# One attention stage of a fused kernel: TensorE's loop over single groups, single buffers for what it reads, and K and V projected later

## The reference, cut to what matters

```python
x = _layernorm(x + _attn(x, x, x, ..., True), ln1_g, ln1_b)
x = _layernorm(x + _attn(x, encoder_output, encoder_output, ..., False), ln2_g, ln2_b)
x = _layernorm(x + _moe(x, router_w, router_b, e_w1, e_b1, e_w2, e_b2), ln3_g, ln3_b)
```

```python
Q = (q_in @ wq + bq).reshape(Bq, Sq, H, HD)
Kp = (k_in @ wk + bk).reshape(Bq, Sk, H, HD)
V = (v_in @ wv + bv).reshape(Bq, Sk, H, HD)
scores = jnp.einsum('bqhd,bkhd->bhqk', Q, Kp) / jnp.sqrt(jnp.float32(HD))
a = jax.nn.softmax(scores, axis=-1)
o = jnp.einsum('bhqk,bkhd->bqhd', a, V).reshape(Bq, Sq, Dm)
return o @ wo + bo
```

## Time and profile before

| | |
|---|---|
| median of 3 runs | 1501.34 us (1499.0 to 1504.86) |
| the profiled execution's own time | 1501.08 us |
| its span, first to last instruction | 1499.4 us |
| mean granted TensorE clock | 0.933 of full |
| busy share of the span: PE, PEld, DVE, ACT, POOL | 86%, 72%, 65%, 66%, 57% |
| attention phase | first values about 24 us, last residual 564 us |
| fused stage | first bias matmul 948 us, last residual 1354 us |

### The profile page before, as it was taken

How to read it: one execution, slowest core, us unless ns; L and a number is a source line. 1 busy time by engine, 2 the same in 40 slices (tenths; PEclk the granted TensorE clock), 3 DMA queues, 4 the chain that set the end, 5 groups by cost and what they waited for, 6 DMA issues and landing times. The chain is left out here.

```text
span 1499.4 us, 59843 instructions
## 1 busy us (share of the span) xinstructions
PE 1284.4 (86%) x23136; PEld 1073.3 (72%) x23136; DVE 969.2 (65%) x2107; ACT 997.0 (66%) x2030; POOL 861.9 (57%) x1340
## 2 busy tenths in 40 slices
PE   5999999989999987679999999157887777895998
PEld 2787887778888776568999999136665556683776
DVE  4787787767878865883555555266877767762332
ACT  1778877768788852986666666166776666772554
POOL 2557766656676753108999987566555554322331
PEclk9999999999999995598999999669999999996999
DMA  3232332322322430522222223242332323212221
GB/s 102 76 103 91 98 105 91 95 87 80 89 80 88 117 90 8 176 64 63 69 68 68 68 67 65 66 106 65 84 89 68 96 64 82 66 31 57 71 70 49
DMA packets 154923, 118.91 MB, mean 79 GB/s; under 512 B 17440, under 2 KB 130592, under 8 KB 154784
## 3 DMA queue, kind: packets, MB, share of 16 engines
q1 hardware_dynamic: 146336, 99.61, 22.6%
q0 software_dynamic: 8448, 17.32, 5.1%
HBM read 78.55 MB, written 38.27 MB: 78 GB/s over the span
## 5 line engine op out<-in xcount | busy, mean ns | idle before, releaser
L831 DVE TENSOR_REDUCE at_mx<-at_ps_s 128x16 f32<-128x1024 f32 x128 | 156.1, 1220 | 106.9 <-PE at_ps_s L560 60.4
L760 ACT ACTIVATE at_pt<-at_ps_t 128x1024 f32<-128x1024 f32 x128 | 130.6, 1020 | 56.3 <-PE at_ps_t L574 55.6
L753 ACT ACTIVATE at_pr<-at_dd 128x1024 f32<-128x1024 f32 x128 | 135.2, 1056 | 34.7 <-DVE at_dd L839 34.6
L2261 ACT ACTIVATE ex_hg<-ex_ps_h,ex_wt 128x128 f32<-128x128 f32 x544 | 154.4, 372 | 1.3 <-PE ex_ps_y L2230 1.2
L2201 POOL DMA_INDIRECT ex_xg<-x,ex_ti x136 | 141.2, 1038 | 23.4 <-issue 21.8
L2282 DVE COPY ex_wt<-experts 128x1156 f32 x136 | 105.0, 774 | 75.7 <-issue 64.3
L839 DVE TENSOR_TENSOR at_dd<-at_ps_s,at_mx 128x1024 f32<-128x1024 f32 x128 | 153.8, 1203 | 0.1
L2221 PE MATMUL ex_ps_h<-ex_xt,ex_wt 128*128 128x128 f32 x1088 | 148.6, 281 | 0.0
L1611 POOL DMA_INDIRECT l_yg<-rows,l_sl x128 | 128.8, 1007 | 33.0 <-issue 30.8
L574 PE MATMUL at_ps_t<-ident,at_pr 128*128 128x128 f32 x1024 | 139.9, 280 | 5.1 <-issue 3.1
L2230 PE MATMUL ex_ps_y<-ex_wt,ex_hg 128*128 128x128 f32 x1088 | 143.6, 275 | 0.4 <-ACT ex_hg L2261 0.4
(11 more groups left out here) (239 smaller groups left out, 3282.9 us busy)
## 6 DMA issues: line engine op xcount, KB each, us to landing
rows<-ex_y SPq DMA_DIRECT2D x136, 64.0 KB
x<-at_ln_out SPq DMA_DIRECT2D x32, 256.0 KB, 3.2
at_kx<-in_xt SPq DMA_DIRECT2D x16, 256.0 KB, 2.8
at_qx<-in_xt SPq DMA_DIRECT2D x16, 256.0 KB, 2.8
at_vin<-in_xt SPq DMA_DIRECT2D x16, 256.0 KB, 2.7
at_xr<-in_x SPq DMA_DIRECT2D x16, 256.0 KB, 3.0
x1t<-at_xt SPq DMA_DIRECT2D x16, 256.0 KB, 3.2
at_kx<-in_ctxt SPq DMA_DIRECT2D x16, 256.0 KB, 2.7
```

The source lines that it names most:

```text
L753: act.activation(pr[:, p], dd[:, p], ACT.Exp, scale=SCALE).then_inc(p_ready, 1)
L760: act.activation(pt[:, 2 * h + p], ps_t[:, :, :, :], ACT.Copy).then_inc(pt_ready, 1)
L831: dve.tensor_reduce(mx[:, p], ps_s[:, :, 4 * p:4 * p + 4, :], AX.X, ALU.max).then_inc(mx_ready, 1)
L2261: ins = act.activation(hg[:, s % 2, f, :], ps_h[s % HB][:, f, :], ACT.Gelu, bias=wt[:, s % HB, B1 + f:B1 + f + 1])
```

## The change

- `kv` becomes two tiles, `kx` and `vin`, each single; `qx`, `kb`, `qb`, `ot`, `z4` and `c.vx` become single. K and V of a group are loaded by two transfers instead of one.
- TensorE's loop is `over_ones`, one step in its body, over g = 2 to 14; unrolled are g = -1, 0, 1 and 15, 16, 17. Its step is rotated (it begins with `project_out` of g-2, `turn`, `scores` of g second half).
- `project_k` is of g+1 instead of g+2. `project_v` is of g instead of g+1, and stands ahead of `scores` of g+1 first half instead of behind it.
- ScalarE: `copy_t` of the first pair is behind `mask_q`; `exponent` of pair (2g+1, 0) is behind `mask_k`; `copy_v` is of g, ahead of `exponent` of (2g+1, 1). VectorE: `recip` of the first half is ahead of `gain_own`. GpSimd: `spread` of the first half is ahead of `fetch_open`. The other moves in their steps are rotations: the same cyclic order with the step's boundary elsewhere.
- SyncE: order x, output, front (four groups ahead instead of five), `x3`, K two ahead, V one ahead.

```diff
+def over_ones(eng, step, first, end, last):
+    for g in range(first, 2):
+        step(At(1, g))
+    with eng.Fori(2, end) as m:
+        step(At(1, m, 0, m))
+    for g in range(end, last):
+        step(At(1, g))
...
-        kv = n.sb("kv", [P, 2, GT])
-        qx = n.sb("qx", [P, 2, GT])
+        kx = n.sb("kx", [P, GT])
+        vin = n.sb("vin", [P, GT])
+        qx = n.sb("qx", [P, GT])
-        kb = n.sb("kb", [P, 2, 2, GT])
-        qb = n.sb("qb", [P, 2, GB, 2, SEQ])
+        kb = n.sb("kb", [P, 2, GT])
+        qb = n.sb("qb", [P, GB, 2, SEQ])
...
+                def load_k(a):
+                    if beyond(a.g, 0):
+                        sp.wait_ge(k_ready, a.g)
+                    sp.dma_start(kx[:, :], layer.kv_src[:, bass.ts(a.place, GT)]).then_inc(in_k, 16)
...
 sync step
-                    if a.shift(2).exists():
-                        load_kv(a.shift(2))
                     if a.shift(1).exists():
                         load_x(a.shift(1))
                     if a.shift(-2).exists():
                         store_tok(a.shift(-2))
-                    if a.shift(5).exists():
-                        load_front(a.shift(5))
+                    if a.shift(4).exists():
+                        load_front(a.shift(4))
                     if a.shift(3).exists():
                         store_x3(a.shift(3))
+                    if a.shift(2).exists():
+                        load_k(a.shift(2))
+                    if a.shift(1).exists():
+                        load_v(a.shift(1))
...
 tensor step
+                    if a.shift(-2).exists():
+                        if a.shift(-1).exists():
+                            pe.wait_ge(vx_ready, g)
+                        else:
+                            pe.wait_ge(y_ready, g - 2)
+                        project_out(a.shift(-2))
+                    if a.shift(-1).exists():
+                        turn(g * 2 - 1, 1, 1)
+                    if a.exists():
+                        scores(a, 1)
...
-                        project_k(a.shift(2))
+                    if a.shift(1).exists():
+                        pe.wait_ge(qb_ready, g + 2)
+                        project_k(a.shift(1))
                     if a.exists():
                         turn(g * 2, 0, 1)
                     if a.shift(-1).exists():
                         widen(g * 2 - 1, 1)
+                    if a.exists():
+                        if a.shift(1).exists():
+                            pe.wait_ge(kb_ready, g + 2)
+                        else:
+                            pe.wait_ge(y_ready, g - 1)
+                        project_v(a)
                     if a.shift(1).exists():
                         scores(a.shift(1), 0)
-                        if a.shift(2).exists():
-                            pe.wait_ge(kb_ready, g + 3)
-                        else:
-                            pe.wait_ge(qb_ready, g + 2)
-                        project_v(a.shift(1))
...
-                over_steps(pe, step, NG - 2)
+                over_ones(pe, step, -1, NG - 1, NG + 2)
...
 scalar step
                     if a.exists():
-                        exponent(g * 2 + 1, 0)
+                        copy_t(g * 2, 0, 0)
                     if a.shift(-1).exists():
                         copy_o(g * 2 - 1, 1)
-                    if a.shift(2).exists():
-                        mask_k(a.shift(2))
+                    if a.shift(1).exists():
+                        mask_k(a.shift(1))
                     if a.exists():
+                        exponent(g * 2 + 1, 0)
                         copy_t(g * 2, 0, 1)
+                        copy_v(a)
```

More of the change, by code:

```diff
@@ L1087, in fused_phase @@
         z4t_ready, qx_ready = n.sem("z4t_ready"), n.sem("qx_ready")
-        in_kv = [n.sem(f"in_kv{i}") for i in range(2)]
+        in_k, in_v = n.sem("in_k"), n.sem("in_v")
         in_x = [n.sem(f"in_x{i}") for i in range(2)]
@@ L1389, in step @@
                     g = a.g
+                    if a.shift(-1).exists():
+                        exponent(g * 2 - 1, 1)
+                        copy_t(g * 2 - 1, 1, 0)
+                    if a.shift(2).exists():
+                        scale_own(a.shift(2))
+                    if a.shift(1).exists():
+                        scale_next(a.shift(1))
                     if a.exists():
@@ L1402, in step @@
                     if a.exists():
-                        exponent(g * 2 + 1, 0)
+                        copy_t(g * 2, 0, 0)
                     if a.shift(-1).exists():
                         copy_o(g * 2 - 1, 1)
-                    if a.shift(2).exists():
-                        mask_k(a.shift(2))
+                    if a.shift(1).exists():
+                        mask_k(a.shift(1))
                     if a.exists():
+                        exponent(g * 2 + 1, 0)
                         copy_t(g * 2, 0, 1)
-                        exponent(g * 2 + 1, 1)
-                    if a.shift(1).exists():
-                        copy_v(a.shift(1))
-                    if a.exists():
-                        copy_t(g * 2 + 1, 1, 0)
-                    if a.shift(3).exists():
-                        scale_own(a.shift(3))
-                    if a.shift(2).exists():
-                        scale_next(a.shift(2))
-                over_steps(act, step, NG - 4)
+                        copy_v(a)
+                over_steps(act, step, NG - 2)
             @block.vector
@@ L1537, in step @@
                     if a.exists():
+                        subtract(g * 2 + 1, 0)
+                    if a.shift(3).exists():
+                        weigh_first(a.shift(3))
+                    if a.exists():
                         maximum(g * 2 + 1, 1)
@@ L1569, in step @@
                         normalise(a, 0)
-                    if a.shift(1).exists():
-                        subtract(g * 2 + 3, 0)
-                    if a.shift(4).exists():
-                        weigh_first(a.shift(4))
                 over_steps(dve, step, NG - 4)
@@ L1633, in step @@
                     g = a.g
-                    if a.shift(3).exists():
-                        fetch(a.shift(3), 0, 1)
-                        fetch(a.shift(3), 1, 2)
-                        fetch(a.shift(3), 2, 3)
-                    if a.shift(-2).exists():
-                        spread(g * 2 - 3, 1)
-                    if a.shift(3).exists():
-                        fetch(a.shift(3), 3, 4)
-                        fetch(a.shift(3), 4, 5)
                     if a.shift(2).exists() or a.shift(1).exists():
@@ L1648, in step @@
                         fetch(a.shift(3), 7, 8)
+                    if a.shift(-1).exists():
+                        spread(g * 2 - 2, 0)
                     if a.shift(4).exists():
@@ L1651, in step @@
                     if a.shift(-1).exists():
-                        spread(g * 2 - 2, 0)
                         add_bias(a.shift(-1))
+                    if a.shift(4).exists():
+                        fetch(a.shift(4), 0, 1)
+                        fetch(a.shift(4), 1, 2)
+                        fetch(a.shift(4), 2, 3)
+                    if a.shift(-1).exists():
+                        spread(g * 2 - 1, 1)
+                    if a.shift(4).exists():
+                        fetch(a.shift(4), 3, 4)
+                        fetch(a.shift(4), 4, 5)
                 pool.wait_ge(bob_ready, 1)
```

99 lines of the change are left out of this document (42 added, 57 removed).

## The result

The changed kernel takes 1488.96 us (median of 4 runs, 1485.52 to 1492.4) against 1503.1 us before (4 runs, 1499.0 to 1511.67): ratio 0.9881, 95% interval 0.9846 to 0.9916. It is faster by 1.2%, by less than half of what I forecast, and 1 us outside my range.

The account below looks back on a forecast made before the run. No engine was full in the fused stage; waits came from TensorE's code fetches and the crawl, with VectorE as floor. 30.6 + 5 - 1.5 = 34 us off 1501.1 gave 1467 us, range 1438 to 1488.

Parts of the forecast that it names:

- The fetches: TensorE's instruction fetches in the fused stage: gone from g = 3 on; 1.2 us a group at the back edge, similar elsewhere.
- single buffers: Tiles made single in the fused stage: new waits ask for readers three or more blocks back, so they cost nothing.
- `scores` beside a gather ... take the same 1.17 us: TensorE's `scores` in the fused stage: no slower beside a gather than without, so only `values` suffers.
- layout: One fused-stage group timed, zero at the end of `subtract` (2g+1, 1): 19.7 us, or 20.3 with some cold clock.
- The crawl is just escaped here: First half's `values`: runs from 2.7 to 4.5 us after the layout's zero, ending as gathers start at 4.5.
- the crawl: Slow weight loads of TensorE's `values` beside gathers, 3.8 us a group before; forecast to move to the second half.
- cold clock: TensorE's clock falling to 0.50 behind the crawl: `project_k` and `turn` 0.9 us more each, taken in one group of five.
- rival with the crawl in both halves: `values` of both halves slowed, clock always cold: 22.8 us a group, 1493 us in all, chance 0.12.
- The term 9 x (23.7 - 20.3) = 30.6 us: Gain in groups 1 to 10 of the fused stage, from 23.7 to 20.3 us each.
- signs of being wrong: `maximum` waiting for `scores` over a microsecond in most groups, or `project_k` waiting for its load, would refute the prediction.
- rival without any crawl: `values` escapes slowing in both halves, in the fused stage: groups of 18.2 us, 1445 us in all, chance 0.27.
- The 1.44 us at the start: Stage's start: K of group 0 projected behind Q, its mask ahead of the first `scores`, 1.44 us later; its load lands before.

Follow-up runs that it names:

- e3: The changed kernel with TensorE's loop of two groups again, all else as changed: 1431.81 us, ratio to before 0.9907.
- e7: The kernel before with 20 more bias matmuls ahead of TensorE's loop, which then touches 7 code blocks instead of 8: 1439.22 us, ratio 0.9905.
- e8: e3 with 44 more bias matmuls ahead of TensorE's loop, which then touches 8 code blocks instead of 7: 1465.71 us, ratio to before 1.011.
- e9: The changed kernel, unchanged, run again on the chip of sets A and C: 1434.23 us, ratio to before 0.991.
- e13: The changed kernel with GpSimd's gathers moved away from `values` (rows 5 to 7 wait for the first half's), on a third chip: 1482.59 us, ratio to before 0.9851.
- e15: The changed kernel, unchanged, run again on a third chip: 1488.62 us, ratio to before 0.9883.
- e14: The changed kernel with GpSimd's indirect gathers replaced by as many plain loads from GpSimd (rows in token order), on a third chip: 1418.3 us, ratio to before 0.9416.
- set D: Runs of e13, e14 and e15 on a third chip, where the kernel before took 1505.9 us (7 runs).

## Why the prediction was wrong

**The fetches** went as forecast: no q8 between 1071 and 1287 us, no "issue" at `turn_z`. By the two-page rule of the Trainium skill ("Runtime: NRT & Kernel Launch", Instruction fetch mechanics) the back edge would still have waited; the traces of after, e3 and e7 disagree with it. My reason, that a one-group body stays resident, holds but was not the point: a two-group body stays resident too when it touches 7 blocks (e3, e7). Their price is about 20 us in all by e7 and e8 on one chip, and the change gains 18.4 there. Without its dead work e7 would stand at 1439.2 - 7.0 = 1432.2 us, beside 1434.1 of the kernel after. So there what the change gains is the fetches, and the new order and the single buffers add nothing that shows. That the block count decides is shown at four positions of one loop, 7, 7, 8 and 8 blocks; where the limit is for other loops it doesn't show.

**The failed step is "`scores` beside a gather ... take the same 1.17 us", and with it the layout's "The crawl is just escaped here".** I had `scores` until 1.6, `values` of a first half at 2.7 to 4.5 us and the gathers at 4.5. In the trace, counted from the same zero, the gathers start at 4.3 to 4.5, `mask_k` ends at -0.5 to -0.7 in eight of ten groups and `scores` start at 0.5 to 0.7 in them, all as laid out. But `values` starts at 2.9 to 3.05, because a gather lies beside these `scores` and they take 1.4 to 1.5 us. The rows of one group, then the same `scores` of e9, where the crawl is weak (the clock is 1.00 in both):

```profile
1147.76 0.94 POOL L1628 DMA_INDIRECT l_yg<-rows,l_sl  x1 [0.31 <-issue]
...
1148.49 1.53 PE L1185 MATMUL l_ps_s<-l_kb,l_qb 32*128 32x128 f32 x32
```
```profile
1118.75 0.94 POOL L1628 DMA_INDIRECT l_yg<-rows,l_sl  x1 [0.30 <-issue]
...
1119.43 1.17 PE L1185 MATMUL l_ps_s<-l_kb,l_qb 32*128 32x128 f32 x32
```

In e9 the layout holds nearly to the letter: `values` starts at 2.63, the gather at 4.44, and the first half escapes. In the first measurement the gather comes 0.8 to 1.5 us behind the start of `values`, not 1.8, and the block takes 3.6 to 5.7 us. The edge is steep: 5.6 to 5.7 us where the gather comes 0.8 to 1.3 us behind, 4.3 where it comes 1.4, and 3.6 where it comes 1.43 to 1.51, with one gather less in the block. From 1060 to 1262 us ten first halves average 4.4 us (5.7 before) and nine second halves 3.6 (2.6 before). I had 1.8 and 5.1. So the crawl moved to the second half as forecast, but only in part, and stayed in the first: about 8 us a group instead of 6.9, nearly the 8.3 of before.

**The rest of the missed 2.2 us a group** isn't separated. I let the cold clock reach `project_k` in one group out of five, and it did so about as often: 2.08 us once in nine groups and 1.5 once. But cold or slowed blocks behind and beside a crawl come in every group, and the layout had few of them: `project_out` takes 1.79 us on average (1.15 in e9), `scores` 1.38 (1.12), with a mean clock of 0.93. How much of this VectorE waits for isn't shown. In sum it is 22.5 us a group, against 20.3 forecast, and near the 22.8 of the rival with the crawl in both halves. The term 9 x (23.7 - 20.3) = 30.6 us measured 9 x 1.2 = 11 us. That rival, 1493 us, was the right one, and I gave it 0.12. Its condition, "with `mask_k` in time the first half escapes", was the same layout. One of the signs of being wrong came true too: in five of nine groups `maximum` waits over a microsecond, four times for `scores` (up to 1.9 us) and once 3.9 us for something that the profile doesn't name.

**Two readings of the profile were too quick.** "`scores` beside a gather ... take the same" was true of one gather in a trace; the rows above and e13 refute it as a rule. And the rival without any crawl (1445 us) rested in part on the Trainium skill ("SBUF — State Buffer", Who interferes with whom), by which TensorE's reads are free of the other engines and of DMA. The gaps are "issue" waits, between instructions, so they don't contradict it; but it doesn't follow that a gather can't slow TensorE, and e15 beside e14 shows that it does.

**Right:** faster, no wait for K's load in the steady groups, VectorE as the floor (at 17.1 us a group in e14, not 18.0), and the single buffers at no cost: TensorE waits for `l_kb` 0.4 us at most. The 1.44 us at the start came as forecast: from `l_bob` to the first `scores` it is 45.67 us (947.46 to 993.13) against 44.23 before (949.11 to 993.34), though not for the reason alone that I gave: I had K's load landing before its use, and TensorE waits 1.7 us for it at 989.5 us, where before it waited 1.5 us for `mask_q`.

**What stays open:** why an indirect gather slows TensorE, what makes the gathers cost 43 us in nine groups on one chip and 4 us on another, and why the gaps begin only with the third of four gathers in e13 but with the first in the earlier trace rows. That it is the chip and not the moment rests on two sets on one chip, 1447.4 and 1446.5 us before; the chip of set D was measured in one set. Gathers with their indices in token order, which would tell the scattered rows from the gather itself, weren't run. A version that spaces the gathers one by one was not tried. No kernel here beats both on every chip: e3 equals the kernel after, and e13 is 0.4% below it on one chip (intervals overlap) and 1.7% above it on another.

## What to carry to other kernels

A loop body near the size at which TensorE's code is still resident can gain or lose some 20 us by where it starts; count the blocks that it touches, or shift it by a few instructions, before the order of work is rewritten for it, and take the shift's own dead work out of the comparison. Indirect gathers of GpSimd can cost time on TensorE, which no row of GpSimd shows, and delay a stage's first group: try plain loads in their place once, to see the price, and compare on more than one chip. An event that a layout by hand lets escape by 0.0 us is a coin toss and not a forecast; give both branches about equal chances.

## What the runs showed of the hardware

- A two-group loop of 1661 to 1663 TensorE instructions isn't fetched again when it touches 7 blocks of 16 KB and is when it touches 8, with 21 to 22 fetches in 100 us.
- Beside a row of indirect gathers TensorE can be down to some four matmuls and their loads every 0.73 us (1108.21 to 1108.94 above), without a fetch. Two plain loads by GpSimd in the middle of `values` do nothing to it: 1.83 us in e14.
- This differs between the sets and their chips: the same kernel takes 1434 and 1489 us, while VectorE's own work in nine groups is the same (155.54 us in e15, 155.63 in e9).
- A gather occupies GpSimd for about 1.0 us, a plain load of the same size for 0.56 us.
